# Two softmax layers: the row maxima are turned on VectorE and copied by DMA into the query operand

## What is computed

```python
# layer 0: 32 heads of 4 channels (two per output head), values of 8 channels
scores = einsum('bhtd,bhsd->bhts', q * hd ** -0.5, k)          # per head 1024 x 1024
attn_w = softmax(scores, axis=-1)
aw = attn_w[:, :, 0] - lam * attn_w[:, :, 1]                   # of each pair of heads
attn = einsum('bhts,bhsd->bhtd', aw, v)                        # then an rms norm and Wo
# layer 1: 16 heads of 8 channels, keys whose x[..., 0] is zero are masked
scores = where(key_mask, einsum('bthd,bshd->bhts', q, k) * scale, -inf)
out = einsum('bhts,bshd->bthd', softmax(scores, axis=-1), v)
```

## Time and profile before

| | |
|---|---|
| median of 3 runs | 2075.88 us (2075.8 to 2077.05) |
| the profiled execution | 2076.24 us, of which span 2074.4 us |
| TensorE busy / VectorE busy / ScalarE busy | 94% / 76% / 67% of the span |
| layer 0's softmax stage | first exponential at 52.9 us, last near 656 us |
| layer 1's softmax stage | first exponential at 760.1 us, last near 1068 us |
| mean granted TensorE clock | 0.981 of full speed |

### The profile page before, as it was taken

One profiled execution on the slowest core, in us unless ns is written; L12 is line 12 of the kernel. 1 busy time (PEld: TensorE's weight loads), 2 busy tenths in 40 slices (PEclk: granted clock), 3 DMA queues, 4 the chain that ended last, 5 costly groups with the idle time before them and its releaser, 6 DMA issues. The chain is left out here.

```text
span 2074.4 us, 43441 instructions
## 1 busy us (share of the span) xinstructions
PE 1955.2 (94%) x17202; PEld 858.4 (41%) x17202; DVE 1574.4 (76%) x2254; ACT 1386.3 (67%) x2761; POOL 208.4 (10%) x388
## 2 busy tenths in 40 slices
PE   8999999999999979999998999999999899999998
PEld 4222222222223422222233666666665344444453
DVE  7999999999995599999946667776774655555553
ACT  4899999999998549899875666666774422222253
POOL 3011111110111330111100000000000200000000
PEclk7999999999999979999999999999999999999999
DMA  3000010110101020101010011110111055555510
GB/s 102 2 24 20 23 31 16 31 25 14 32 11 28 1 57 12 30 19 41 8 29 6 13 26 26 26 26 16 23 23 39 14 128 121 122 122 120 120 45 21
DMA packets 76041, 82.63 MB, mean 40 GB/s; under 512 B 23744, under 2 KB 58560, under 8 KB 71888
## 3 DMA queue, kind: packets, MB, share of 16 engines
q1 hardware_dynamic: 74896, 79.06, 16.0%
q0 software_dynamic: 528, 0.43, 0.1%
q10 hardware_dynamic: 432, 0.56, 0.1%
HBM read 62.98 MB, written 2.42 MB: 32 GB/s over the span
## 5 line engine op out<-in xcount | busy, mean ns | idle before, releaser
L1069 DVE TENSOR_REDUCE a0nm<-ps 128x2 f32<-128x1024 f32 x512 | 586.9, 1215 | 11.0 <-PE ps L936 8.8
L1047 ACT ACTIVATE a0p<-ps 128x512 f32<-128x512 f32 x1024 | 544.1, 599 | 60.4 <-PE ps L956 43.6
L970 PE MATMUL ps<-a0p,a0vst 128*32 128x256 f32 x4096 | 328.0, 392 | 27.4 <-ACT a0p L1047 14.0
L1069 DVE TENSOR_REDUCE a1nm<-ps 128x2 f32<-128x1024 f32 x256 | 294.7, 1217 | 7.2 <-PE ps L936 6.3
L1047 ACT ACTIVATE a1p<-ps 128x512 f32<-128x512 f32 x512 | 275.6, 596 | 34.4 <-PE ps L956 25.5
L956 PE MATMUL ps<-a0qm,a0k 32*128 32x512 bf16 x1024 | 277.3, 387 | 0.0
L2157 ACT ACTIVATE ex_s<-ps 128x512 f32<-128x512 f32 x128 | 76.4, 597 | 253.0 <-PE ps L2112 253.0
L936 PE MATMUL ps<-a0k,a0q 32*128 32x512 bf16 x1024 | 203.5, 395 | 17.9 <-DVE a0nm L1069 15.7
L2246 DVE TENSOR_TENSOR ex_su<-ex_s,ps 128x512 f32<-128x512 f32 x128 | 88.0, 688 | 114.2 <-PE ps L2116 113.7
L1757 PE MATMUL ps<-cak,caq 64*128 64x512 f32 (+3 forms) x768 | 171.3, 521 | 2.1 <-DVE canm L1909 2.1
L970 PE MATMUL ps<-a1p,a1vst 128*32 128x256 f32 x2048 | 164.1, 393 | 6.4 <-ACT a1p L1047 5.5
(11 more groups left out here) (327 smaller groups left out, 2495.0 us busy)
## 6 DMA issues: line engine op xcount, KB each, us to landing
ex_wb<-ex_w_dram SPq DMA_DIRECT2D x62, 512.0 KB, 6.2
xc_res<-car_dram SPq DMA_DIRECT2D x32, 256.0 KB, 4.2
xc_res<-a0rec SPq DMA_DIRECT2D x15, 256.0 KB
a0q<-a0parts_sb SPq DMA_DIRECT2D x95, 32.0 KB, 2.0
a1q<-a1parts_sb SPq DMA_DIRECT2D x94, 32.0 KB
a0k<-a0parts_sb SPq DMA_DIRECT2D x90, 32.0 KB, 2.0
a1k<-a1parts_sb SPq DMA_DIRECT2D x84, 32.0 KB
f2wg<-in_ex_gate SPq DMA_DIRECT2D x32, 64.0 KB, 1.8
```

What stands on the lines that cost most here:

```text
L970: last = pe.matmul(R.ps[32 * j:32 * j + 32, 6, cols], vst[:, g, s, j * HG // 4, :], p[:, s % 2, j, cols], start=(g == 0 and s == 0 and hal ...
L1047: act.activation(p[:, s % 2, e, :], R.ps[:, score_bank(n), :], ACT.Exp).then_inc(exp_done, 1)
L1069: dve.tensor_reduce(nm[:, u % 2, tb, 2 - 2 * z:4 - 2 * z, hf], R.ps[:, bank:bank + 2, :], X_AXIS, ALU.max, negate=True).then_inc(bank_free, 1)
```

## The change

The maxima no longer pass through TensorE, PSUM and `qm`.

- `join` becomes an element-wise minimum; GpSimd's `split` has four operations instead of five and puts the three parts (and a fourth, always zero) into a 128 x 64 tile `mt`.
- VectorE transposes `mt` in 32 x 32 blocks into `mr` (128 x 64 bf16, two buffers). This is the new `turn`.
- SP then copies `mr` into the spare rows of `A.q` itself, for the 512 query columns of the unit, by eight DMAs (`maxima_rows`): each reads 32 partitions of 32 elements and writes 8 partitions, four pieces of 32 elements each. The score matmuls read `A.q`.
- Before a unit's scores TensorE waits on `rows_in`, that is, on the landing of these eight DMAs.
- The spare rows must be zero while the maxima are made, so every load of q of the groups from 4 on gets one more DMA that writes zeros into them (`load_queries`).
- The maxima run 9 slots ahead instead of 6 (`LEAD`), the join moves to the end of step 3 and the turn to the end of step 4.
- The places in SP's list: `maxima_rows` of units 0, 1 and 2 behind the loads of groups 1 to 3; that of unit 2n+3 behind L842 of iteration n; that of unit 2n+4 at the very end of iteration n.

```diff
@@ class Attn
-        self.spare = (7, 15, 23)
+        self.spare_step = rows // 4
+        self.spare_rows = slice(7, 128, self.spare_step)
...
+def load_queries(A, idx, slot, queue):
+    load_rows(A, idx, slot, 0, queue)
+    if idx >= 4:
+        queue.dma_start(A.q[A.spare_rows, slot, :, :], A.zero_rows[:]).then_inc(A.ld[slot], 16)
+
 def load_group(A, idx, slot, queue):
-    load_rows(A, idx, slot, 0, queue)
+    load_queries(A, idx, slot, queue)
     load_rows(A, idx, slot, 1, queue)
@@ softmax_stage
+    LEAD = 9
-    qm = sb("qm", [128, 2, RT, CW], BF16)
-    mt = sb("mt", [128, 4, 4, ROWS], BF16)
+    mt = sb("mt", [128, 4, 4, 4], BF16)
+    mr = sb("mr", [128, 2, 2, 32], BF16)
+    A.zero_rows = sb("zero_rows", [512 // ROWS, RT, T], BF16)
...
-        slots = [(u + 1 + n // 16, n % 16) for n in (6 + 2 * s, 7 + 2 * s)]
+        slots = [(u + 1 + n // 16, n % 16) for n in (LEAD + 2 * s, LEAD + 1 + 2 * s)]
     def turns_at(u, s):
-        return s == 6 and u + 1 < UNITS
+        return s == 4 and u + 1 < UNITS
@@ on_sp
+        def maxima_rows(u):
+            _k, chunk_i, _g, slot = place(u)
+            sp.wait_ge(mt_step, 3 * u + 3)
+            for i in range(4):
+                for pair in range(2):
+                    rows = slice(7 + 64 * pair, 64 + 64 * pair, 8) if RT == 1 else A.spare_rows
+                    to = q[rows, slot, pair % RT, chunk_i * CW:chunk_i * CW + CW].rearrange("p (t i r) -> p t i r", t=4, i=4)
+                    sp.dma_start(to[:, :, i, :], mr[32 * i:32 * i + 32, u % 2, pair, :]).then_inc(rows_in, 16)
+
+        for u in range(3):
+            maxima_rows(u)
         for n in range(2 * PAIRS - 1):
...
             sp.dma_start(rec_dram[c].rearrange("r (a t) -> (r a) t", a=16), packed[:, c, :]).then_inc(rec_out[c], 16)
+            maxima_rows(2 * n + 3)
             sp.wait_ge(rec_out[c], times)
...
                 load_group(A, 2 * kk, kk % 2 * 2, sp)
-                load_rows(A, 2 * kk + 1, kk % 2 * 2 + 1, 0, sp)
+                load_queries(A, 2 * kk + 1, kk % 2 * 2 + 1, sp)
...
+            if 2 * n + 4 < UNITS:
+                maxima_rows(2 * n + 4)
@@ on_pool, split(u): four operations in place of five
-            pool.wait_ge(max_ready, u + 1)
-            if u:
-                pool.wait_ge(bank_full, filled("turn", u - 1))
+            pool.wait_ge(mt_step, 3 * u + 1)
...
+            pool.tensor_tensor(part[:, 2], m1[:], part[:, 1], ALU.subtract).then_inc(mt_step, 1)
@@ on_pe
-        def turn(u):
-            pe.wait_ge(mt_ready, u + 1)
-            out = bf16_bank(wait_bank("turn", u))
-            for tb in range(4):
-                for r in range(RT):
-                    last = pe.transpose(out[:, r, tb * 128:(tb + 1) * 128],
...
             pe.matmul(R.ps[:, score_bank(n), :], k[rows, place(u)[3], rt, s * 128:(s + 1) * 128],
-                      qm[rows, u % 2, rt, :], start=True, stop=True).then_inc(p2_full, 1)
+                      q[rows, place(u)[3], rt, place(u)[1] * CW:(place(u)[1] + 1) * CW], start=True, stop=True).then_inc(p2_full, 1)
...
         for u in range(UNITS):
-            pe.wait_ge(bank_free, emptied("turn", u))
+            pe.wait_ge(rows_in, 128 * (u + 1))
...
-                if turns_at(u, s):
-                    turn(u + 1)
@@ on_dve
-            dve.tensor_reduce(m0[:], nm[:, u % 2], X_AXIS, ALU.min).then_inc(max_ready, 1)
-        def merge(u):
-            _k, chunk_i, _g, slot = place(u)
-            dve.wait_ge(bank_full, filled("turn", u))
-            if u >= 2:
-                dve.wait_ge(exp_done, u * 32 - 32)
-            t0 = chunk_i * CW
-            dve.tensor_tensor(qm[:, u % 2], q[:, slot, :, t0:t0 + CW], bf16_bank(dve_bank("turn", u)),
-                              ALU.add).then_inc(bank_free, 1)
+            dve.tensor_tensor(m0[:], nm[:, u % 2, :, :, 0], nm[:, u % 2, :, :, 1], ALU.min).then_inc(mt_step, 1)
+        def turn(u):
+            dve.wait_ge(mt_step, 3 * u + 2)
+            if u >= 2:
+                dve.wait_ge(rows_in, 128 * (u - 1))
+            dve.transpose(mr[:, u % 2].rearrange("p a r -> p (a r)"), mt[:].rearrange("p h k t -> p (h k t)")).then_inc(mt_step, 1)
...
+        reduce(1, 0)
         join(0)
-        for i in range(4):
+        for i in range(1, 3):
             reduce(1, i)
-        merge(0)
-        for i in range(4, 6):
+        turn(0)
+        for i in range(3, LEAD):
             reduce(1, i)
...
-                if s == 5 and u < UNITS - 1:
-                    join(u + 1)
                 if slots[1]:
                     reduce(*slots[1])
+                if s == 3 and u + 1 < UNITS:
+                    join(u + 1)
                 if turns_at(u, s):
-                    merge(u + 1)
+                    turn(u + 1)
```

More of the change, by code:

```diff
@@ L166, in __init__ @@
         self.n_pool_loads = 4 * self.row_tiles
+        self.zero_rows = None
         self.inited = [nc.alloc_semaphore(name + "inited0"), nc.alloc_semaphore(name + "inited1")]
@@ L780, in ahead @@
     def ahead(u, s):
-        slots = [(u + 1 + n // 16, n % 16) for n in (6 + 2 * s, 7 + 2 * s)]
+        slots = [(u + 1 + n // 16, n % 16) for n in (LEAD + 2 * s, LEAD + 1 + 2 * s)]
         return [x if x[0] < UNITS else None for x in slots]
     def turns_at(u, s):
-        return s == 6 and u + 1 < UNITS
-    turns = [("max", 0, i) for i in range(16)] + [("max", 1, i) for i in range(4)] + [("turn", 0)]
-    turns += [("max", 1, i) for i in range(4, 6)]
-    for u in range(UNITS):
-        for s in range(8):
-            turns += [("max", *x) for x in ahead(u, s) if x]
-            turns += [("turn", u + 1)] if turns_at(u, s) else []
+        return s == 4 and u + 1 < UNITS
+    turns = [("max", u, i) for u in range(UNITS) for i in range(16)]
     turns += [("spread",)]
@@ L818, in score_bank @@
         return (4, 5, 7)[n % 3]
-    def bf16_bank(b):
-        return R.ps[:, b, :].bitcast(BF16).rearrange("p (r t) -> p r t", r=2)[:, 0:RT, :]
     def on_sp(sp):
@@ L865, in on_pool @@
         pool.memset(zero[:], 0.0).then_inc(pool_step, 1)
-        pool.wait_ge(pool_step, 3)
+        pool.memset(A.zero_rows[:], 0.0).then_inc(pool_step, 1)
+        pool.wait_ge(pool_step, 4)
         def stage_v(g):
@@ L877, in split @@
         def split(u):
-            pool.wait_ge(max_ready, u + 1)
-            if u:
-                pool.wait_ge(bank_full, filled("turn", u - 1))
-            none, done = zero[:, 0:4, 0:4], 3 + u * 4
-            pool.tensor_tensor(mt[:, :, :, A.spare[0]], m0[:], none, ALU.add).then_inc(pool_step, 1)
+            part, none, done = mt[:].rearrange("p h k t -> p k h t"), zero[:, 0:4, 0:4], 4 + u * 3
+            pool.wait_ge(mt_step, 3 * u + 1)
+            pool.tensor_tensor(part[:, 0], m0[:], none, ALU.add).then_inc(pool_step, 1)
             pool.wait_ge(pool_step, done + 1)
-            pool.tensor_tensor(m1[:], m0[:], mt[:, :, :, A.spare[0]], ALU.subtract).then_inc(pool_step, 1)
-            pool.wait_ge(pool_step, done + 2)
-            pool.tensor_tensor(mt[:, :, :, A.spare[1]], m1[:], none, ALU.add).then_inc(pool_step, 1)
+            pool.tensor_tensor(m1[:], m0[:], part[:, 0], ALU.subtract).then_inc(pool_step, 1)
+            pool.tensor_tensor(part[:, 1], m0[:], part[:, 0], ALU.subtract).then_inc(pool_step, 1)
             pool.wait_ge(pool_step, done + 3)
-            pool.tensor_tensor(m2[:], m1[:], mt[:, :, :, A.spare[1]], ALU.subtract).then_inc(pool_step, 1)
-            pool.wait_ge(pool_step, done + 4)
-            pool.tensor_tensor(mt[:, :, :, A.spare[2]], m2[:], none, ALU.add).then_inc(mt_ready, 1)
+            pool.tensor_tensor(part[:, 2], m1[:], part[:, 1], ALU.subtract).then_inc(mt_step, 1)
         def divide(n):
@@ L928, in p1_slot @@
                 by_pool = 0 if slot else A.n_pool_loads
-                pe.wait_ge(ld[slot], 16 * ((kk // 2 + 1) * A.n_loads - by_pool))
+                pe.wait_ge(ld[slot], 16 * ((kk // 2 + 1) * A.n_loads + kk // 2 - by_pool))
                 if u == 0:
@@ L937, in p1_slot @@
                           k[rows, slot, rt, hf * CW:(hf + 1) * CW], start=True, stop=True).then_inc(bank_full, 1)
-        def turn(u):
-            pe.wait_ge(mt_ready, u + 1)
-            out = bf16_bank(wait_bank("turn", u))
-            for tb in range(4):
-                for r in range(RT):
-                    last = pe.transpose(out[:, r, tb * 128:(tb + 1) * 128],
-                                        mt[:].rearrange("p b h w -> p b (h w)")[:, tb, r * 128:(r + 1) * 128],
-                                        R.identb[:])
-            last.then_inc(bank_full, 2)
         def score(u, s, e):
@@ L987, in on_pe @@
                 A.among_maxima[i]()
-        for i in range(4):
-            p1_slot(1, i)
-        turn(0)
-        for i in range(4, 6):
+        for i in range(LEAD):
             p1_slot(1, i)
@@ L1068, in reduce @@
             bank = dve_bank("max", u, i)
-            dve.tensor_reduce(nm[:, u % 2, tb, 2 - 2 * z:4 - 2 * z, hf], R.ps[:, bank:bank + 2, :],
```

(1 more changed line is left out.)

4 lines of the change are left out of this document (2 added, 2 removed).

## The result

The changed kernel takes 2552.91 us (median of 4 runs, 2551.6 to 2555.64) where the kernel before takes 2076.47 beside it: a ratio of 1.2295, interval 1.2273 to 1.2316. It is slower, as forecast, but by 476 us and not by 129, far above the range.

What follows compares the result with a forecast made beforehand. VectorE was taken as the bound at 18.9 us a unit, ScalarE 5% behind. Layer 0's +62 and layer 1's +67 made +129 on 2076.24 us: 2206 us, range 2115 to 2275.

Steps and rivals of the forecast that it cites:

- Sum: Both layers added: 62 + 67 = +129 us, giving 2206 us; new memsets and waits on landings taken as hidden.
- TensorE's ... transposes ... I cost them at nothing: Four or eight transposes a unit leave TensorE; said to lie beside VectorE's work, so counted as zero.
- SP's chain: Before each unit TensorE waits for eight DMAs issued by SP: 7 x 0.60 + 2.0 + 0.9 = 7.1 us.
- plain pairs: Two units without loads: 39.2 us for 37.83 in layer 0, 39.5 for 38.6 in layer 1.
- those with loads: Pairs whose next even unit's rows wait behind SP's loads: +7.4 us each in layer 0, +15.2 in layer 1.
- VectorE's side: VectorE loses merge (0.41) and hole (0.18), gains a 0.1 us transpose; unit 18.4 us, at most 30 us gained.
- the ceiling: Most that VectorE's relief can give in layer 1: 0.9 us for each of 16 units, 14 us.
- Cheap issues: Rival: SP issues at 0.36 us, landing 1.4, chain 4.8 us; 2123 us, or 2100 to 2150; chance 0.19.
- nearly free ones: Rival: SP issues at 0.05 us, chain 3.25 us; about +17, 2093 us; chance 0.04.
- those of 0.70: Upper end for SP's issues: 0.70 us each, landing 3.0, chain 8.8 us; 2288 us.
- rival (2): Small pieces make SP's copies dear to issue and land; 2288 us, or above 2255; chance 0.11.
- Rival (4): The turn set the pace; without it units run at ScalarE's 17.95 us, 52 us gained; 2061 us; chance 0.04.

Runs made afterwards that it cites:

- e1_swap: Changed kernel, still nine slots ahead, with the two halves of each pair of maxima slots in the other order: 2223.13 us, ratio to before 1.0709.
- e9_pool10: Changed kernel with row copies issued by GpSimd, maxima ten slots ahead, join after step 2, turn one maximum later: 2067.44 us, ratio to before 0.9954.

## Why the prediction was wrong

**The step that failed** stands under "Sum": "All else ... lies beside other work". In it the lead of nine was costed at nothing; it appeared only as an earlier demand for k in layer 1. It is the largest effect of the change, +330 us (2552.9 against 2223.1): each half step takes 1.97 us and not 1.56 at 1.2 GHz, and the clock stays at 1.2 GHz through layer 0. The step "TensorE's ... transposes ... I cost them at nothing" looked at TensorE's work only as time saved, where four traces show the clock to rise behind just these transposes once rows collide. A moved matmul also gets a new neighbour, and which rows of the array the two share was never asked. It could have been: the rows of four heads follow from `rows_of` and the parity from `slot_of`, and TensorE's timeline of before shows four matmuls beginning within 0.01 us.

**The clock.** The forecast let it fall after pauses and return, as it does at 55 to 60 us and in e1_swap. The changed kernel has hardly a pause in layer 0 (1.2 us on the copied rows) and runs at 1.2 GHz for a millisecond. Every case in the forecast had a clock near full in layer 0; so none reaches beyond 2288, and the range ends at 2275. Slower, as forecast, it is by SP's chain alone, for 147 of the 476 us; the rest has the same sign for a reason that the forecast did not have.

**SP's chain: right, sizes near.** Eight issues take 5.0 us: 0.583 each, and (5.00 - 0.583) / 7 = 0.631 from one start to the next, where the forecast's sum has 0.60. The first exponential of layer 0 is at 57.31 (forecast 57.8). With the collision away, 2223 against 2206: layer 0 is +78.7 by the table against 62, layer 1 +63.8 against 67. The 14 pairs of e1_swap's layer 0 take 596.3 us, where six of 45.2 and eight of 39.2 make 584.8: the plain pairs measure 40.3 in the mean (forecast 39.2) and those with loads 45.7 (forecast 45.2), since in them too TensorE waits and the clock falls. Behind the last of these rows of SP layer 0 takes 9.2 us more than before (forecast 1.7), ahead of the first 2.8 (forecast 4.8). In layer 1 of the changed kernel the plain pairs are 39.1 to 41.3 and those with loads 54.0 and 54.6 (forecast 39.5 and 53.8), and its first exponential lies 1195.09 - 1129.93 = 65.2 us behind its first query load, where it was 760.13 - 723.45 = 36.7: +28.5 (forecast +29.7).

**VectorE's side: right in layer 0.** A transpose of 0.1 was forecast and measures 0.16; the unit of 18.4 without a late row is 18.55 in e9_pool10. In layer 1 the ceiling was too high: 0.9 us a unit was forecast at the most, and the pairs of e9_pool10 give back 0.9 in two units.

**The rivals.** Cheap issues, nearly free ones and those of 0.70 are excluded by the 0.583 us. The condition "above 2255" of rival (2) is met by 2552.91 in number only: its mechanism, dear issues and landings, is not what happened. Rival (4), faster without the turn, gave it 52 us through ScalarE's pace; what VectorE frees is 0.73 us a pair of layer 0, and 8.6 us in all is what e9_pool10 gains on the kernel before.

## What to carry to other kernels

Where small matmuls share the array by rows, the order in which they meet is part of the schedule: a lead changed by one, or an odd number in place of an even one, can put each beside the one that uses its rows. Print, for every neighbouring pair, the rows they use, before and after a change of lead. And when copies go through a queue that also carries loads, give them the queue that is free when they become ready, and enough lead for the whole chain: here that turned +7% into -0.5%.

## What the runs showed of the hardware

- Matmuls of 32 rows that share their rows with a neighbour begin 0.4 us later at 1.2 GHz and 0.2 us later at 2.4. A pair of units loses some 14 us by it at 1.2 GHz (63.65 against 49.9, an estimate from 32 half steps of 1.56 us) and 0.8 at 2.4 (38.63 against 37.83). With the collision, the low clock costs a pair 25 us (63.65 against 38.63).
- TensorE was at 1.2 GHz for a millisecond with the collision, busy 577 of 580 us. The Trainium skill (TensorE: Matmul & The Clock Gate, "Part 1: The HAM clock gate") says that "the default state is throttled, and activity releases the throttle". Here a TensorE that the profile shows busy without a gap was not released, so the busy share alone doesn't tell which clock to expect.
- With the collision, one kernel's time spread from 2124.78 to 2386.35 us, through the moment at which the clock rose. In all four traces that have it, it rose within 2.6 us of the start of a unit's four 128 x 128 transposes.
- One issue of 32 pieces of 64 bytes took 0.583 us on SP and 0.541 on GpSimd (medians); the block transpose of 128 x 64 bf16 on VectorE took 0.234 in the changed kernel and 0.245 in e9_pool10.
